# Late stack fills moved to GpSimd, the first stack's transfers dealt out anew, two rows of VectorE's order exchanged, and bf16 filler products on TensorE

## What is computed

```python
qkv = layernorm(x) @ w_qkv                    # 2048 x 384, split into q, k, v: 16 heads of 8
q, k = rope(q), rope(k)
attn = softmax(where(causal, q @ k.T * 8 ** -0.5, lowest))
x = x + concat_heads(attn @ v) @ w_out
h = layernorm(x)
gate = softmax(h @ router_W.T + router_b)     # 6 experts, the top 2 kept and renormalised
x = x + (h @ base_W.T + base_b) + shared(h) + sum_e gate_e * routed_e(h)
```

## Time and profile before

| | |
|---|---|
| median of three runs | 319.71 us |
| the profiled execution | 319.8 us |
| its span, first to last instruction | 318.1 us |
| mean granted clock of TensorE | 0.973 |
| PE busy | 285.8 us, 90% |
| ACT busy | 269.6 us, 85% |
| DVE busy | 146.3 us, 46% |
| POOL busy | 57.5 us, 18% |

### The profile page before, as it was taken

One profiled execution on the slowest core, in us unless ns is written; L12 is line 12 of the kernel. 1 busy time (PEld: TensorE's weight loads), 2 busy tenths in 40 slices (PEclk: granted clock), 3 DMA queues, 4 the chain that ended last, 5 costly groups with the idle time before them and its releaser, 6 DMA issues.

```text
span 318.1 us, 7501 instructions
## 1 busy us (share of the span) xinstructions
PE 285.8 (90%) x3006; PEld 103.8 (33%) x3008; DVE 146.3 (46%) x425; ACT 269.6 (85%) x300; POOL 57.5 (18%) x129
## 2 busy tenths in 40 slices
PE   7948883989899989899999998999999999999896
PEld 2613241222223422123313313443533333433353
DVE  6775596468875376956241003651000514101064
ACT  8567584779999798999999999999999999999700
POOL 0485141031330300403003020101001010110100
PEclk9966998799999999999999999999999999999999
DMA  6333137000550000160000100000100000000000
GB/s 173 112 93 92 26 103 190 10 1 2 152 148 0 23 15 1 35 165 2 0 3 0 36 2 2 0 3 2 35 2 3 2 2 0 2 19 2 3 0 16
DMA packets 15400, 11.75 MB, mean 37 GB/s; under 512 B 2033, under 2 KB 14178, under 8 KB 15362
## 3 DMA queue, kind: packets, MB, share of 16 engines
q1 hardware_dynamic: 14866, 10.90, 12.6%
q10 hardware_dynamic: 432, 0.20, 0.2%
q0 software_dynamic: 64, 0.13, 0.1%
HBM read 3.88 MB, written 1.05 MB: 16 GB/s over the span
## 4 chain that ended last, share of the span: by engine, by line
PE 37%; ACT 22%; DVE 21%; issue 15%; DMA 2%; SPq 1%; DVEq 1%; POOL 0%; ACTq 0%; POOLq 0%
ACT pbuf L588 22%; PE po L962 17%; PE ps L940 9%; PE pm L978 3%; DVE rest L665 3%; DMA xs<-x_dram 2%; PE ps L1082 2%; DVE rot L672 2%; DVE absmax L696 1%; PE pm L1021 1%; PE pm L1015 1%; DVE oq L647 1%; DVE rot L659 1%; DVE rest L682 1%; PE pm L972 1%
## 5 line engine op out<-in xcount | busy, mean ns | idle before, releaser
L588 ACT ACTIVATE pbuf<-ps 128x1024 f32<-128x1024 f32 (+1 forms) x280 | 253.9, 1068 | 24.6 <-PE ps L940 24.2
L962 PE MATMUL po<-pbuf,va 128*9 128x256 f32 (+3 forms) x1792 | 146.7, 433 | 9.3 <-DVE oq L647 7.0
L940 PE MATMUL ps<-qst,kst 64*128 64x256 bf16 (+3 forms) x896 | 97.7, 303 | 8.1 <-ACT pbuf L588 3.4
L537 POOL TENSOR_SCALAR_AFFINE_SELECT pbuf<-pbuf 128x256 f32<-128x256 f32 (+1 forms) x104 | 48.9, 492 | 231.6 <-ACT pbuf L588 230.4
L940 PEld LDWEIGHTS ps<-qst,kst 64*128 64x128 bf16 x896 | 30.3, 95 | 104.0 <-ACT pbuf L588 77.2
L962 PEld LDWEIGHTS po<-pbuf,va 128*9 128x9 f32 x1792 | 35.6, 90 | 66.7 <-issue 42.8
L647 DVE STREAM_TRANSPOSE oq<-po 128x256 f32<-128x256 f32 (+1 forms) x24 | 12.9, 536 | 84.7 <-PE po L962 84.4
L665 DVE TENSOR_TENSOR rest<-pm,sinT 32x512 f32<-32x512 f32 x16 | 11.0, 687 | 0.3
L978 PE MATMUL pm<-xnT,wqkv 128*128 128x512 f32 x16 | 9.0, 644 | 1.9 <-DVEq L812 1.3
L1082 PE MATMUL ps<-kst 128*128 128x512 bf16 x44 | 10.5, 379 | 0.2 <-issue 0.2
L806 DVE COPY lowT<-pm 113x512 f32<-113x512 f32 (+1 forms) x5 | 2.9, 585 | 16.6 <-PE pm L1029 16.6
(11 more groups left out here) (115 smaller groups left out, 184.6 us busy)
## 6 DMA issues: line engine op xcount, KB each, us to landing
qst<-parts SPq DMA_DIRECT2D x18, 128.0 KB, 2.4
kst<-parts SPq DMA_DIRECT2D x18, 128.0 KB, 2.5
xs<-x_dram SPq DMA_DIRECT2D x4, 256.0 KB, 4.1
cosT<-rope_c_dram SPq DMA_DIRECT2D x4, 256.0 KB, 4.4
sinT<-rope_s_dram SPq DMA_DIRECT2D x4, 256.0 KB, 5.6
out_dram<-xs SPq DMA_DIRECT2D x3, 256.0 KB, 2.3
kst<-parts SPq DMA_DIRECT2D x11, 64.0 KB, 2.1
qst<-parts SPq DMA_DIRECT2D x8, 64.0 KB, 2.0
```

Source lines behind the costliest of these rows:

```text
L537: ins = nc.gpsimd.affine_select(out=edge, in_=edge, compare_op=ALU.is_ge, fill=0.0, base=0, pattern=[[0, edge.shape[1]], [1, P]], channel_ ...
L588: nc.scalar.activation(probs[:, :, 0:width], ps[:, u % NS, :, 0:width], ACT.Exp, scale=SCALE).then_inc(exp_ready, 1)
L940: ins = nc.tensor.matmul(ps[:, u % NS, e, place:place + n], side(kst, e)[:, g * 2 + pair, key:key + P], side(qst, e)[:, g * 2 + pair, q:q ...
L962: ins = nc.tensor.matmul(po[32 * j:32 * j + DH + 1, q0:q0 + n], va[:, kt, g * GH + j, :], pbuf[:, u % NPB, at:at + n], start=blk["first"] ...
```

## The change

- **Fills.** ScalarE now fills `kst` of chunks 0, 1 and 2 and `qst` of chunk 0, all before unit 0. GpSimd fills `qst` of chunk 1 right at its start (one MEMSET of 2048 float32 a partition), and the remaining three (queries of chunk 2, keys and queries of chunk 3) as twelve MEMSETs of 512 a partition, one ahead of each of units 24 to 35 in its program. The waits on `filled` change to match.
- **Loads.** Chunk 0's cosine and sine tables come in two halves; the second halves and chunk 1's tables stand behind chunk 1's rows.
- **First stack.** All six key transfers and the last query transfer are SP's, queries 0, 3 and 4 ACT's, queries 1 and 2 GpSimd's.
- **VectorE's order.** The flag of prep 0 is set ahead of rope for prep 1's queries. The moments of chunk 1 (L614, L617 of before) stand where they stood.
- **GpSimd's inverse square root.** One Newton step and one third-order step (ten instructions) in place of three Newton steps (twelve).
- **Filler products.** They read filled `kst` columns in bf16: six and four around the bound's product, three ahead of the first scores, two after each of units 0 to 3 (into `pm`).
- **Waits.** The bound's product waits for the first half of V only; the first values of each group wait for both.
- **Places.** In the first piece B and K1 move from 5 to 3. In the fourth, BD and the ten jobs from K1 to R move two units later; in the fifth, jobs A to X and F do; in the sixth, W1 to F move one or two units earlier.

```diff
-FIRST_BY_SP = (("K", 0), ("K", 1), ("K", 2), ("Q", 0), ("K", 3), ("K", 4), ("Q", 5))
-FIRST_BY_ACT = (("Q", 1), ("Q", 3), ("Q", 4))
-FIRST_BY_POOL = (("Q", 2), ("K", 5))
+FIRST_BY_SP = (("K", 0), ("K", 1), ("K", 2), ("K", 3), ("K", 4), ("K", 5), ("Q", 5))
+FIRST_BY_ACT = (("Q", 0), ("Q", 3), ("Q", 4))
+FIRST_BY_POOL = (("Q", 1), ("Q", 2))
...
+LATE_FILLS = ([("Q", 0.0, 2 * TC + t) for t in range(TC)]
+              + [("K", ONE_ONE, 3 * TC + t) for t in range(TC)] + [("Q", 0.0, 3 * TC + t) for t in range(TC)])
+LATE_FILL_UNITS = range(FIRST_UNIT[2], FIRST_UNIT[2] + len(LATE_FILLS))
+FILLS_BY_ACT = (2, 3, 4, 4)
+FILLS_BY_POOL = (0, 1, 1 + TC, 1 + 3 * TC)
...
-WARM_BOUND = 3
-WARM_FLAG = 1
+WARM_BOUND = 6
+WARM_FLAG = 4
+WARM_KEYS = 3
+WARM_UNITS = (2, 2, 2, 2)
...
-    (1, 1, 2, 5, 5, 6),
+    (1, 1, 2, 3, 3, 6),
...
-            load_chunk(0)
-            load_chunk(1)
+            load_rows(0)
+            sp.dma_start(idf[:, :], ident).then_inc(ident_in, 16)
+            sp.dma_start(wqkv[:, :, :], w_qkv).then_inc(qkv_in, 16)
+            load_rope(0, 0, HALF_CH)
+            load_rows(1)
+            load_rope(0, HALF_CH, CH)
+            load_rope(1)
...
+            def fill(stacked, value, first, tiles):
+
+                nc.gpsimd.memset(stacked[:, :, first * P:(first + tiles) * P].bitcast(F32),
+                                 value).then_inc(filled_by_pool, 1)
+
             nc.gpsimd.memset(va[:, :, :, DH:DH + 1], 1.0).then_inc(zeroed, 1)
+            fill(qst, 0.0, TC, TC)
...
             for u, unit in enumerate(UNITS):
+                if u in LATE_FILL_UNITS:
+                    stacked, value, tile = LATE_FILLS[LATE_FILL_UNITS.index(u)]
+                    fill(kst if stacked == "K" else qst, value, tile, 1)
...
-            fill_queries(1)
+            fill_keys(2)
...
-            fill_keys(2)
...
-                if u + 1 == FIRST_UNIT[1]:
-                    fill_queries(2)
...
-            rope_second("Q")
             dve.wait_ge(bound_full, 1)
             set_flag(0, pm[:, :])
+            rope_second("Q")
             rope_second("K")
...
-                    if NEW_PREP[FIRST_UNIT.index(u)] == 2:
-                        last = slice((NC - 1) * CH, NC * CH)
-                        nc.vector.memset(kst[:, :, last].bitcast(F32), ONE_ONE).then_inc(filled_last, 1)
-                        nc.vector.memset(qst[:, :, last].bitcast(F32), 0.0).then_inc(filled_last, 1)
...
-            keep_warm(WARM_BOUND, wqkv[:, 0, :], xnT[:, 0, :])
+            hot = kst[:, 0, CH:CH + P], kst[:, 0, CH:2 * CH]
+            pe.wait_ge(filled, FILLS_BY_ACT[1])
+            keep_warm(WARM_BOUND, *hot)
             pe.wait_ge(const_in, 16 * 4)
-            pe.wait_ge(v_ready, 2)
+            pe.wait_ge(v_ready, 1)
             pe.wait_ge(bound_ready, 1)
             sum_bound(pm[:, :]).then_inc(bound_full, 1)
-            keep_warm(WARM_FLAG, wqkv[:, 0, :], xnT[:, 0, :])
+            keep_warm(WARM_FLAG, *hot)
...
+                    if p == 0:
+                        keep_warm(WARM_KEYS, *hot)
                     wait_for_queries(pe, p)
                 if u in NEW_KEYS_UNIT:
                     wait_for_keys(pe, NEW_KEYS_UNIT[u])
                 scores(u)
+                if u < len(WARM_UNITS):
+                    keep_warm(WARM_UNITS[u], *hot, pm[:, :])
```

More of the change, by code:

```diff
@@ L362, in at_flag, with plain_third_order @@
             return engine.value_load(flag[0:1, p:p + 1], min_val=0, max_val=1)
-        def newton(engine, then, v, r, s):
-            for _ in range(3):
-                then(engine.tensor_tensor(s, r, r, ALU.mult))
-                then(engine.tensor_tensor(s, s, v, ALU.mult))
-                then(engine.tensor_scalar(s, s, -0.5, 1.5, ALU.mult, ALU.add))
-                then(engine.tensor_tensor(r, r, s, ALU.mult))
+        def plain_third_order(engine, then, v, r, s, w):
+            then(engine.tensor_tensor(s, r, r, ALU.mult))
+            then(engine.tensor_tensor(s, s, v, ALU.mult))
+            then(engine.tensor_scalar(s, s, -0.5, 1.5, ALU.mult, ALU.add))
+            then(engine.tensor_tensor(r, r, s, ALU.mult))
+            then(engine.tensor_tensor(s, r, r, ALU.mult))
+            then(engine.tensor_tensor(s, s, v, ALU.mult))
+            then(engine.tensor_scalar(w, s, 0.375, -1.25, ALU.mult, ALU.add))
+            then(engine.tensor_tensor(w, w, s, ALU.mult))
+            then(engine.tensor_scalar(w, w, 1.875, None, ALU.add))
+            then(engine.tensor_tensor(r, r, w, ALU.mult))
         def third_order(engine, then, v, r, s):
@@ L387, in inverse_sqrt @@
             if engine is nc.gpsimd:
-                newton(engine, then, v, r, s)
+                plain_third_order(engine, then, v, r, s, w)
             else:
@@ L407, in wait_for_fill @@
         def wait_for_fill(engine, p):
[L409 to L412 removed]
+            engine.wait_ge(filled, FILLS_BY_ACT[chunk(p)])
+            if FILLS_BY_POOL[chunk(p)]:
+                engine.wait_ge(filled_by_pool, FILLS_BY_POOL[chunk(p)])
         def wait_for_keys(engine, p):
[L416 to L421 removed]
+            engine.wait_ge(keys_in[p], 16 * len(SLOTS))
         def wait_for_queries(engine, p):
             if p == 0:
[L426 to L428 removed]
+                engine.wait_ge(queries_in[0], 16 * (len(SLOTS) - len(FIRST_BY_POOL) - len(FIRST_BY_ACT)))
+                engine.wait_ge(queries_by_pool, 16 * len(FIRST_BY_POOL))
                 engine.wait_ge(queries_by_act, 16 * len(FIRST_BY_ACT))
@@ L492, in _ @@
             stack(2)
-            load_chunk(2)
+            load_rows(2)
+            load_rope(2)
             stack_maxima(2)
             stack(3)
-            load_chunk(3)
+            load_rows(3)
+            load_rope(3)
             stack_maxima(3)
@@ L1077, in row_maxima, with keep_warm @@
                 pe.nop()
-            def keep_warm(times, left, right):
+            def keep_warm(times, left, right, into=ps[:, 1, 1, :]):
                 for _ in range(times):
-                    nc.tensor.matmul(ps[:, 1, 1, :], left, right, start=True, stop=True)
+                    nc.tensor.matmul(into, left, right, start=True, stop=True)
             pe.wait_ge(warm_ready, 1)
```

39 lines of the change are left out of this document (12 added, 27 removed), and 6 rows, old and new, of the table PLACES.

## The result

| | before | after |
|---|---|---|
| median of four runs, us | 319.38 (318.76 to 320.12) | 311.22 (311.14 to 312.49) |
| the profiled execution, us | 319.8 | 311.1 |
| its span, us | 318.1 | 309.4 |
| mean granted clock | 0.973 | 0.999 |

The ratio is 0.975, with a 95% interval of 0.972 to 0.978. The gain is 8.2 us by the medians and 8.7 by the two profiled executions.

A forecast was written before the change was run, and what follows sets the result against it. ScalarE's exponentials bound the kernel, so gains come only where ScalarE starves, at 18 to 28 and 49 to 60 us. 5.3 + 0.8 - 0.3 = 5.8 us off 319.8 gives 314.0, range 312.0 to 317.0.

The forecast's parts named there:

- The middle, 5.3: Around 50 us: without VectorE's two fills ahead of the copy of `po`, 5.3 us gained, 3.9 VectorE's time, 1.4 clock.
- Rival C: Middle: the clock falls all the same or another wait replaces the fills; only 2.5 to 3.9 gained, 316.3 us, chance 0.10.
- The start, 0.8: Stage from 18 to 28 us: earlier loads and flag, partly countered by job B, gain 0 to 1.4 us, taken 0.8.
- (a): Start, loads: chunk 1's rows land earlier with 256 KB less ahead of them; 0 to 1.86 us, taken 1.2.
- (b): Start, flag: VectorE waits for the bound's sum with no work in between, 0.4 us on its chain; unit 0 1.1 to 1.6 earlier.
- (c): Start, unit 10: it waits for prep 1's keys, whose six transfers follow VectorE's split and move 0.8 us earlier.
- (d): Start: job B behind unit 3 delays units 4 and 5; keys no earlier at the lower clock, 0.8 us survive at the higher.
- rival B: Start gains nothing, since B's new place and a clock still at 1.2 GHz hold the first values and keys; 314.8 us, chance 0.19.
- Contention, -0.3: Third piece's first normalisation: GpSimd's late fills beside VectorE slow it; 0.3 us charged, bounds 0 to 1.6.
- GpSimd's fills: Twelve late MEMSETs of 512: 0.651 to 1.1 us each, taken 0.7; free to TensorE up to 1.13 us a fill.
- rival E: Late fills cost far more, so masks of units 32 to 35 come late; 324.4 us at 2.0 a fill, chance 0.06.
- The late places, 0: Pieces four to six: jobs moved by one or two units where ScalarE is 97% busy gain 0, at most 0.5 either way.

The follow-up runs named there:

- V alone: The changed kernel with the fourth piece's job places as before, except job V at 33 instead of 31: 312.13 us.

## Why the prediction was right and wrong

**What bounds it** was right in its two stages and wrong in one sentence. "A gain can come only from the stages where ScalarE starves" took 97% busy from 112 to 300 us as full. The 3% are 5 us, much of it in waits of 0.2 to 0.4 us such as those shown above, and an edit that moves jobs is aimed at these.

**The middle, 5.3: right.** ScalarE's unit 27 came 5.17 us closer to unit 10 (6.53 against 1.36), 5.1 booked, and 0.7 more followed by unit 36, 0.2 booked. The clock's share was 1.9 rather than 1.4 and VectorE's 4.0, 3.9 booked: the kernel with 22 fillers in TensorE's wait shows it. Rival C needed a clock that falls in a 1.6 us gap; the gap was 1.30 and the clock stayed at 1.00.

**The start, 0.8: right in sign, 1.4 in size where the clock held, 0.2 in the change's execution where it fell.** (a) gave more than 1.2. The rows landed before VectorE was free, the whole 1.86 us went, and TensorE's first projections took back 0.37: rope starts 1.4 earlier (9.55 against 10.95). (b) was right: 0.4 booked, 0.38 read, 0.37 won when undone. Unit 0 came 2.03 us earlier, not 1.1 to 1.6. (c) had the keys leave 0.8 us earlier, and they did (25.48 before):

```profile
24.63 3.80 SPq L470 DMA_DIRECT2D kst<-parts  x6
```

The last of them landed 0.94 us earlier (30.87 before, 29.93 after), near the 0.8. But the keys were not what unit 10 waited for. I took PEld's 0.76 us for a wait of TensorE, which was in a projection until the scores could start. What sets unit 10 is the order on TensorE ahead of it: the scores that wait for the queries started 0.54 us earlier (26.32, 26.86 before), and from there to T's turning it took 1.09 us instead of 1.91 (27.41 - 26.32, 28.77 - 26.86), since the values between ran at 0.84 instead of 1.44. The two make the 1.36 us. So 0.8 of the start's gain is this clock directly.

(d) was wrong at the full clock. B's place brakes nothing there: B ran at 23.61, as I said, but values ran at 0.84, and the whole stage came forward. The 0.8 I took was a middle between a clock that falls (0) and one that holds (1.4 was my upper end), and no execution is such a middle. Whether fillers hold the clock I had called open: without them it fell in all six executions, with them it held in five of the change's nine. So rival B's conditions, a low clock and early B, came apart: the low clock takes the gain, B's place does not.

**Contention, -0.3: no loss seen.** The first normalisation took 1.49 us beside masks and fills, 1.27 beside masks alone (before), and the same four operations took 1.11 at 6.87, with GpSimd idle. So VectorE is held there, by up to 0.22 us more than before. TensorE waited 1.29 us for the rows, no longer than before (1.53), and ScalarE's lead stays at 7.26 us from unit 36 to unit 107. The Trainium skill (SBUF — State Buffer, Who interferes with whom) has the later of two instructions that need the shared pair stand still for the whole length of the other. In the middle the times above agree with it in kind. At the start the long MEMSET ended at 3.08 (1.21 + 1.87), not near 5.9, ahead of VectorE's small steps, so no run tests it there.

**GpSimd's fills** were cheaper than both my bounds, 0.48 to 0.60 us, so rival E was further off than I had it.

**The late places, 0: the step that failed.** The prediction put them at nothing because ScalarE is 97% busy there. They gave 1.4 us, nearly three times my bound of 0.5, and the runs show it both ways (undone in the change, done alone in before). With the old places the change's two executions at 1.000 took 312.46 and 312.71, inside the range. The start and the middle, each 0.6 short, had used up most of the range below the forecast, and this term carried the time out of it. In the fourth piece two waits of ScalarE, 0.34 and 0.38, are gone, which is its 0.7; in the fifth two of 0.36 and 0.28. My reading, which is not shown: a job's place within one or two units decides whether TensorE is ahead again when the next one comes. In the profile after, at 130 us, TensorE gets through two units without a job in 1.51 us where ScalarE needs 1.81, so it gains 0.15 a unit, and after a job product of 1.12 us it needs some seven units. Two jobs four units apart then both stall ScalarE. That fits V's wait, which shrank when V moved; but V alone gained nothing, so it is at most part of it. Which jobs of the fifth piece remove its two waits was not tested.

By terms: 1.4 + 5.9 + 0 + 1.4 = 8.7, against 0.8 + 5.3 - 0.3 + 0. The start and the middle were each booked 0.6 too low, the late places 1.4 too low, and the 0.3 of contention did not show.

## What to carry to other kernels

A busy share of 97% over a long window is not a bound: multiply the missing 3% by its length, list the small waits, and look at which of them the moved jobs stand in front of. Give a chance to several small gains adding up, instead of booking each at zero. Read the granted clock of each execution before pricing a part of an edit: the same kernel led by 1.36 or by 0.22 us at unit 10, as the clock held or fell, and a variant that lost the gain may have lost only the clock. And take a wait from the row of the engine that waits: idle time of the weight loads is not idle time of TensorE.
